# Moving a reflect-padding pass and its stores from one block of a kernel into the next, where other engines run beside it

## What is computed

```python
def gn(v, G=32, eps=1e-05):            # x: (4, 64, 56, 56)
    g = v.reshape(B, G, C // G, H, W)
    m, s = g.mean((2, 3, 4), keepdims=True), g.var((2, 3, 4), keepdims=True)
    return ((g - m) / sqrt(s + eps)).reshape(v.shape)

x1, x2, x3 = conv1x1(gn(x), w1c, b1c), conv1x1(gn(x), w2c, b2c), conv1x1(gn(x), w3c, b3c)
x2p = pad(x2, 3, mode='reflect')                      # 56x56 -> 62x62
diff = stack([x1 - x2p[:, :, dy:dy + H, dx:dx + W] for dy, dx in OFFS])   # 49 offsets
y = relu(bn(diff)); y = relu(bn(cw1 @ y)); wgt = softmax(cw2 @ y + cw2_b)  # over the 49 offsets
x3p = pad(x3, 3, mode='reflect')
out = sum(x3p[:, :, dy:dy + H, dx:dx + W] * wgt[:, :, k] for k, (dy, dx) in enumerate(OFFS))
x = x + out
```

## Time and profile before

| | |
|---|---|
| median of 3 runs | 1950.81 us (1948.31 to 1952.43) |
| the profiled execution: its time, its span | 1950.62 us, 1948.7 us |
| busy: PE, DVE, ACT, POOL | 1691.5, 1200.2, 1176.5, 696.9 us |
| first block, from start to barrier | 0 to 62 us |
| convolution's block, first subtraction | 62.00 us |
| first product of VectorE | 135.00 us |
| x3's stores issued, window loads issued | 57.06 us, 96.39 us |

### The profile page before, as it was taken

How to read it: one execution, slowest core, us unless ns; L and a number is a source line. 1 busy time by engine, 2 the same in 40 slices (tenths; PEclk the granted TensorE clock), 3 DMA queues, 4 the chain that set the end, 5 groups by cost and what they waited for, 6 DMA issues and landing times. The chain is left out here.

```text
span 1948.7 us, 33831 instructions
## 1 busy us (share of the span) xinstructions
PE 1691.5 (87%) x13143; PEld 622.7 (32%) x13143; DVE 1200.2 (62%) x1798; ACT 1176.5 (60%) x1605; POOL 696.9 (36%) x401
## 2 busy tenths in 40 slices
PE   4468778778765789999999999999897999999998
PEld 1011111111112434443433443344353334433333
DVE  3139999999985666666666666566265435453333
ACT  2799989989942445444444454444464556565664
POOL 0798978978856310000000000000130214332222
PEclk9799999999987689999999999999987999999999
DMA  2121211211221210000000000100121000010000
GB/s 98 82 101 48 84 37 48 84 44 41 84 95 70 87 34 16 16 15 15 16 16 13 14 15 16 46 15 16 22 79 32 8 5 8 8 41 8 8 10 9
DMA packets 27712, 73.27 MB, mean 38 GB/s; under 512 B 6968, under 2 KB 16184, under 8 KB 26160
## 3 DMA queue, kind: packets, MB, share of 16 engines
q1 hardware_dynamic: 27424, 70.31, 11.3%
q10 hardware_dynamic: 144, 0.96, 0.1%
HBM read 47.84 MB, written 13.62 MB: 32 GB/s over the span
## 5 line engine op out<-in xcount | busy, mean ns | idle before, releaser
L1362 DVE TENSOR_REDUCE at_mpart<-at_ps_m 128x1 f32<-128x384 f32 (+3 forms) x800 | 396.1, 556 | 167.8 <-PE at_ps_m L1072 167.3
L1215 ACT ACTIVATE at_prob<-at_ps_s 128x896 f32<-128x896 f32 x336 | 305.0, 917 | 317.3 <-PE at_ps_s L1090 309.4
L411 POOL TENSOR_TENSOR cm_diff<-front 128x1792 f32<-128x1792 f32 x98 | 320.5, 3274 | 68.9 <-POOLq L113 38.8
L477 DVE TENSOR_TENSOR cm_prod<-cm_ps_ev,win 128x1792 f32<-128x1792 f32 x168 | 333.0, 2018 | 5.3 <-ACT cm_ps_ev L531 1.3
L1881 ACT ACTIVATE ge_hid<-ge_ps,ffn 128x448 f32<-128x448 f32 x448 | 249.7, 634 | 122.1 <-PE ge_ps L1748 122.1
L1111 PE MATMUL at_ps_a<-at_prob,win 128*64 128x448 f32 x1344 | 292.0, 555 | 0.0
L1090 PE MATMUL at_ps_s<-vh,front 64*128 64x448 f16 x1344 | 253.6, 353 | 13.8 <-ACT at_prob L1215 7.8
L1090 PE MATMUL at_ps_s<-vl,front 64*128 64x448 f16 x1344 | 253.1, 352 | 0.0
L642 PE MATMUL cm_ps_acc<-cm_prod,cst 128*32 128x504 f32 x1456 | 197.4, 616 | 60.2 <-DVE cm_prod L477 26.9
L1010 POOL TENSOR_TENSOR attn<-attn 64x448 f32<-64x448 f32 x28 | 31.6, 1127 | 502.1 <-DMA attn<-attn 502.1
L1725 PE MATMUL ge_ps<-ge_hid,ffn 128*64 128x448 f32 x896 | 194.1, 554 | 0.5 <-DVE ge_part L2059 0.4
(11 more groups left out here) (228 smaller groups left out, 1964.2 us busy)
## 6 DMA issues: line engine op xcount, KB each, us to landing
win<-x_dram SPq DMA_DIRECT2D x28, 868.0 KB
at_rden<-rden_dram SPq DMA_DIRECT2D x28, 224.0 KB, 3.3
x_dram<-win SPq DMA_DIRECT2D x4, 962.0 KB
conv_out<-cm_cout SPq DMA_DIRECT2D x28, 112.0 KB, 3.9
win<-x SPq DMA_DIRECT2D x2, 1568.0 KB, 13.3
t_dram<-front SPq DMA_DIRECT2D x2, 1568.0 KB, 7.3
attn<-attn SPq DMA_DIRECT2D x28, 112.0 KB, 2.3
front<-t_dram SPq DMA_DIRECT2D x2, 1568.0 KB, 9.2
```

The lines of the kernel that those rows point to most:

```text
L411: pool.tensor_tensor(diff[:, s % ND, 0:n, :].rearrange("p n (r c) -> p n r c", c=W), a.rearrange("p n (r c) -> p n r c", c=W), b, ALU.subt ...
L477: v.tensor_tensor(halves_of(s)[:, hs, :, 0:CH].rearrange("p s (r c) -> p s r c", c=W), ev.rearrange("p s (r c) -> p s r c", c=W), window_o ...
L1215: act.activation(prob_of(s)[0:w, 0:a, :], ps_s[0:w, (s + 1 - par) % 2, 0:a, 0:CH], ACT.Exp).then_inc(exp_done, 1)
L1362: v.tensor_reduce(mpart[0:w, a, part:part + 1], ps_m[0:w, j % RB, 0:rough_columns(e)], AX.X, ALU.max).then_inc(rough_max, 1)
```

## The change

Five edits. (1) `x3`'s twelve mirror copies and the clearing of its last four columns leave VectorE's list in the first block and stand in the convolution's block, behind its two memsets and ahead of the first `running`. (2) The four stores of `x3` move with them: SyncE issues them in the second block, once `x3_padded` is raised. (3) `x2`'s mirror copies stay in the first block, but most are made while the last chunks of the 1x1 convolutions still run: sides of rows 0 to 47 and the top rows once chunk 5's `x2` is out, the sides of the last 8 rows and the bottom rows once chunk 6's is. (4) TensorE gets nine matmuls whose result nobody reads, six behind the transposition of `cw1` and three behind the matmul of the group means. (5) ScalarE gets an activation of one column as soon as `cst` is there, which brings its table load with it.

```diff
@@ conv_prepare
-                sp.wait_ge(padded, 1)
-                for b in range(B):
-                    dst = bass.AP(tensor=x3_dram.tensor, offset=b * NH * SP * STAGE,
-                                  ap=[[STAGE, 4], [SP * STAGE, NH], [4 * STAGE, 2], [1, STAGE]])
-                    sp.dma_start(dst, x3st[32 * b:32 * b + 32, :, :]).then_inc(x3_sent, 16)
                 sp.wait_ge(tok_in, 16)
...
-                v.wait_ge(evac_done, 4 * NCH)
-                x3v = x3st[:, :, 0:PADDED].rearrange("p s (r c) -> p s r c", c=WP)
                 x2v = x2p[:, :].rearrange("p (r c) -> p r c", c=WP)
-                v.memset(x3st[:, :, PADDED:STAGE], 0.0)
+                LATE = PAD + (NCH - 1) * ROWS
+
+                def sides(first, last):
+
+                    for d in range(PAD):
+                        for a, b in ((d, 2 * PAD - d), (WP - 1 - d, WP - 1 - 2 * PAD + d)):
+                            ins = v.tensor_copy(x2v[:, first:last, a], x2v[:, first:last, b])
+                    return ins
+
+                v.wait_ge(evac_done, 4 * (NCH - 2) + 2)
+                link(sides(PAD, LATE))
                 for d in range(PAD):
-                    for a, b in ((d, 2 * PAD - d), (WP - 1 - d, WP - 1 - 2 * PAD + d)):
-                        v.tensor_copy(x3v[:, :, PAD:PAD + H, a], x3v[:, :, PAD:PAD + H, b])
-                        ins = v.tensor_copy(x2v[:, PAD:PAD + H, a], x2v[:, PAD:PAD + H, b])
-                link(ins)
+                    v.tensor_copy(x2v[:, d, :], x2v[:, 2 * PAD - d, :])
+                v.wait_ge(evac_done, 4 * (NCH - 1) + 2)
+                link(sides(LATE, PAD + H))
                 for d in range(PAD):
-                    for a, b in ((d, 2 * PAD - d), (HP - 1 - d, HP - 1 - 2 * PAD + d)):
-                        ins = v.tensor_copy(x3v[:, :, a, :], x3v[:, :, b, :])
-                        v.tensor_copy(x2v[:, a, :], x2v[:, b, :])
-                ins.then_inc(padded, 1)
+                    v.tensor_copy(x2v[:, HP - 1 - d, :], x2v[:, HP - 1 - 2 * PAD + d, :])
...
+                act.wait_ge(c_in, 16)
+                act.activation(first[:, :], vec("b1"), ACT.Identity, bias=vec("b2"))
                 act.wait_ge(bn_ready, 1)
...
+                def keep_running(times):
+
+                    for _ in range(times):
+                        pe.matmul(psx[:, 1, 3, 0:CH], mat("ident"), cst[:, 0:CH], start=True, stop=True)
+
                 pe.transpose(psx[:, 1, 0, 0:128], cwt[:, :], mat("ident")).then_inc(cw_turned, 1)
+                keep_running(6)
                 pe.wait_ge(moments, 1)
                 pe.matmul(psx[:, 0, 0, 0:4], mat("pair_mean"), mom[:, :, :].rearrange("p t m -> p (t m)"),
                           start=True, stop=True).then_inc(grouped, 1)
+                keep_running(3)
@@ conv_main
+                sp.wait_ge(x3_padded, 1)
+                for b in range(B):
+                    dst = bass.AP(tensor=x3_dram.tensor, offset=b * NH * SP * STAGE,
+                                  ap=[[STAGE, 4], [SP * STAGE, NH], [4 * STAGE, 2], [1, STAGE]])
+                    sp.dma_start(dst, x3st[32 * b:32 * b + 32, :, :]).then_inc(x3_sent, 16)
                 sp.wait_ge(x3_sent, 64)
...
                 v.memset(hid[96:128, 1, :, :], 0.0).then_inc(lanes_done, 1)
                 v.memset(rden_d[:, :, :], 0.0).then_inc(lanes_done, 1)
+                x3v = x3st[:, :, 0:PADDED].rearrange("p s (r c) -> p s r c", c=WP)
+                v.memset(x3st[:, :, PADDED:STAGE], 0.0)
+                for d in range(PAD):
+                    for a, b in ((d, 2 * PAD - d), (WP - 1 - d, WP - 1 - 2 * PAD + d)):
+                        ins = v.tensor_copy(x3v[:, :, PAD:PAD + H, a], x3v[:, :, PAD:PAD + H, b])
+                ins.then_inc(x3_sides, 1)
+                v.wait_ge(x3_sides, 1)
+                for d in range(PAD):
+                    for a, b in ((d, 2 * PAD - d), (HP - 1 - d, HP - 1 - 2 * PAD + d)):
+                        ins = v.tensor_copy(x3v[:, :, a, :], x3v[:, :, b, :])
+                ins.then_inc(x3_padded, 1)
                 for T in TURNS:
```

More of the change, by code:

```diff
@@ L60, with conv_prepare @@
     ["b1", "b2", "b3a", "b3b", "g1", "t1", "m1", "v1", "g2", "t2", "m2", "v2", "cw2b", "cw2b3", "mhalf"])}
-def conv_prepare(nc, x, consts, tok_c, cst, tok, x1, x2p, x3st, x3_dram, x3_sent):
+def conv_prepare(nc, x, consts, tok_c, cst, tok, x1, x2p, x3st):
     with ExitStack() as ctx:
@@ L84, in conv_prepare @@
         tmp = sb("cp_tmp", [128, 4])
+        first = sb("cp_first", [128, 1])
         psx = ctx.enter_context(nc.psum_tensor("cp_psx", [128, 2, 4, BANK], F32))
@@ L100, in conv_prepare @@
         evac_done = sem("cp_evac_done")
-        padded = sem("cp_padded")
         CUTS = (slice(0, 4 * CH), slice(4 * CH, PIX))
@@ L238, in _, with conv_main @@
                     ins.then_inc(conv_done, 1)
-def conv_main(nc, x, cst, front, win, x3_dram, x3_sent, conv_out, tres_in, last_in, early_added):
+def conv_main(nc, x, cst, front, win, x3st, x3_dram, x3_sent, conv_out, tres_in, last_in, early_added):
     with ExitStack() as ctx:
@@ L294, in conv_main @@
         pool_prod_done = sem("cm_pool_prod_done")
+        x3_sides = sem("cm_x3_sides")
+        x3_padded = sem("cm_x3_padded")
         N = NCH * STEPS
@@ L2203, in build @@
             x3st = win_flat[:, 0:2 * STAGE].rearrange("p (s n) -> p s n", s=2)
-            conv_prepare(nc, x, conv_c, tok_c, cst, tok, front[:, 0:PIX], front[:, PIX:PIX + PADDED], x3st, x3_dram,
-                         x3_sent)
-            conv_main(nc, x, cst, front, win, x3_dram, x3_sent, conv_out, tres_in, last_in, early_added)
+            conv_prepare(nc, x, conv_c, tok_c, cst, tok, front[:, 0:PIX], front[:, PIX:PIX + PADDED], x3st)
+            conv_main(nc, x, cst, front, win, x3st, x3_dram, x3_sent, conv_out, tres_in, last_in, early_added)
         tres = tokens_of_front(front)
```

## The result

The changed kernel takes **1965.1 us** (median of 4 runs, 1961.61 to 1967.9) against 1951.62 of four runs before: 1.0071 times as long, with a 95% interval of 1.0057 to 1.0085. That is 13.5 us slower. The profiled execution took 1961.61 us, with a span of 1959.6.

What follows compares the result with a forecast made beforehand. The prediction took VectorE as bound from the first product on, and the window's data chain ahead of it. First product +15.4 and restart 0.8 made +16.2 on 1950.62: 1966.8 us, between 1963.5 and 1971 (1952 to 1971 for 8 in 10).

Steps and rivals of the forecast that it cites:

- S: Time SyncE issues the first store of x3: 57.06 in the kernel before, forecast at 73.4 us.
- the compute chain: From GpSimd's first subtraction through ScalarE's first exponential to VectorE's first product: 73.0 us from block start.
- the first law: Data chain of x3's stores and window loads: first product no earlier than S + 77 us (75.3 to 77.9).
- Taking turns: In the convolution's block, one VectorE copy passes per GpSimd subtraction until subtraction 5 ends: S = 73.4; chance 0.72.
- the burst case: Rival: x3's copies wait for GpSimd only once per group; S = 60.5, whole 1953.2 us; chance 0.12.
- the free case: Rival: x3's copies don't wait for GpSimd at all; S = 57.0, whole 1949.7 us; chance 0.09.
- My doubt about them: Whether x3's column copies take turns with GpSimd; if only the six rows do, S = 72.5 instead of 73.4.
- Block start: GpSimd's first subtraction in the convolution's block: forecast 52.2 us (51.5 to 53.5) instead of 62.00.
- The waking: Extra matmuls and early activation before the 1x1 convolutions: last evacuation 2.3 us earlier (1.0 to 3.0).
- Handovers: Six copies let in between GpSimd's first six subtractions: 0.7 us added to their 19.3.
- the leftovers: Copies left after subtraction 5, the semaphore and six rows, passing freely on VectorE before the stores: 1.2 us.
- The restart: TensorE back at the slow clock after idling before the first product: 0.8 us added (0 to 3).

Runs made afterwards that it cites:

- e1: The changed kernel, but GpSimd's first subtraction waits until x3's copies are made; median 1948.43 us, ratio 0.9996 to the kernel before.
- e2: The changed kernel, but GpSimd makes only its first two subtractions before x3's copies are done; one execution, 1954.34 us.
- e3: The changed kernel, with x3's clearing and copies ahead of the block's two memsets on VectorE; one execution, 1967.78 us.
- e4: The changed kernel, with x3's twelve copies written as four instructions of the same elements; median 1957.26 us, ratio 1.0039 to the kernel before.
- e8: The changed kernel, with 24 unread matmuls on TensorE ahead of the first product's sums; one execution, 1963.72 us.
- e6: The changed kernel, with x3's copies back in the first block and only the stores in the second; median 1946.44 us, ratio 0.9977 to the kernel before.
- e5: The kernel before, with only the nine extra matmuls and the early activation added; median 1947.84 us, ratio 0.9984.
- e7: e6 with the top rows stored and the first window loaded before the rest, staging tile at win's other end; median 1941.57 us, ratio 0.9958.
- e9: e7 with only the last eight rows of x3 mirrored in the second block, in three merged copies; median 1940.87 us, ratio 0.9954.

## Why the prediction was right

**The frame.** The product starts at S + 77 or at block start + 73, whichever is later. In seven kernels the window decided, in four the compute chain:

| kernel | S | behind S | block start | behind it |
|---|---|---|---|---|
| after | 71.42 | **76.95** | 50.89 | 97.48 |
| e1 | 55.26 | **77.00** | 55.31 | 76.95 |
| e2 | 59.24 | **76.86** | 50.97 | 85.13 |
| e3 | 71.46 | **77.27** | 50.92 | 97.81 |
| e4 | 64.06 | **77.00** | 50.63 | 90.43 |
| e8 | 71.33 | **77.10** | 50.78 | 97.65 |
| e6 | 52.55 | **77.07** | 52.58 | 77.04 |
| e5 | 53.71 | 77.91 | 58.64 | **72.98** |
| e7 | 54.16 | (stores cut) | 54.19 | **72.98** |
| e9 | 50.79 | (stores cut) | 50.81 | **73.68** |

(The kernel before, at 77.94 and 73.00, makes the fourth.) In e1 and e6 the store and the block's start fall together: the product comes 77 behind both, where the compute chain takes 73, and its row names the DMA. So the first law isn't the compute chain in disguise. The 77 had been put together from a rate and a count without any row for the fourth load's landing; it held to 0.3.

**Taking turns.** This was the step with the rivals, and it held in kind and nearly in size. Six column copies ended behind six subtractions, the rows passed when GpSimd ran dry, and zero, two, four and six turns gave S = 55.26, 59.24, 64.06 and 71.42. So the burst case (S = 60.5) and the free case (57.0) fall with the trace of the changed kernel, and e1 to e4 exclude that something else held the copies. All six column copies waited, one subtraction each. My doubt about them, drawn from their slow pace, was wrong; it had been priced at 0.9 us. By the Trainium skill (VectorE: DVE Perf Modes, What auto-detection actually checks) a copy from SBUF to SBUF whose outermost dimension is even takes a 2-port mode, and in such a mode it contends with GpSimd for a port pair that whichever issues first holds for the whole instruction (SBUF — State Buffer, Who interferes with whom). The trace agrees, with six waits of six.

**Sizes.** Forecast +16.2 to the 25th product, measured +14.24, and 13.5 between the medians. The terms:

- Block start, 52.2 forecast, 50.89 measured, 0.6 outside its bound of 51.5. The waking had been taken at 2.3 between 1.0 and 3.0, for fear of the clock falling again before the convolutions. It gave 3.12 at the last evacuation, which began at 49.44 (52.56 before). e5 gives 3.36 for both chains. The barrier had been put 0.8 behind the last evacuation; it took 0.29 (50.60 to 50.89), so the 0.77 that stood between the stores' issue and the barrier before was no constant of the barrier. Together 1.3 of the 2.0 missing from S.
- Handovers: 0.7 had been added for six copies let in between; the six subtractions took 19.45 against 19.3, so 0.15. This is 0.5 more. The last 0.15 of the 2.0 is in the leftovers, 1.08 us for 1.2.
- The restart, 0.8 forecast, 0.87 measured. e8 removes it by keeping TensorE busy and so shows the cause. That the size came out so well is luck: the other kernels that stood still lose 0.58 (e3), 1.14 (e1), 1.27 (e4), 1.58 (e2) and 1.59 (e6) up to the 25th product, and not the more the longer they stood (e6 3.98 us, the changed kernel 18.00). What sets it is open.
- The range: the bounds named in the prediction's sum add up to 1962.7 to 1971.2, not to 1963.5 to 1971. The median, 1965.1, lies in both. The profiled execution, 1961.61, lies in neither; of the 5.2 us between it and 1966.8, some 2.0 are S and 3.2 the shorter stretch from attention on, which the sum had as unchanged.

**Where the early block went.** The 11.1 us are real, and e5, e6, e7 and e9 bring 3.4, 5.4, 7.8 and 10.5 of such gains to the first product. In the changed kernel the compute chain would have been ready for the product long before 148.37, and stood still for 18.00 us.

Two things the working had loose. It put the stall at "more like 15"; it was 18.00, since the running maximum is further into the compute chain than assumed. In e9 it came 14.18 behind the block's start without being held up by the copies; in the changed kernel, at 71.31, it was 6.2 late for that, which leaves 148.37 - (50.89 + 73.0 + 6.2) = 18.3. And the profiled execution's span rose by 10.91 only, because attention ran shorter in it; the marks ahead of attention, +14.14, are nearer to the 13.5 between the medians.

## What to carry to other kernels

Work moved to run "beside" another engine is not hidden when the two share a lock: read from the trace what each short instruction took beside the neighbour's long ones, and count the instructions, since here each of them paid a turn as long as the neighbour had work (all but one pair), and not each element. Before moving the start of a block, work out every chain that ends at the first instruction that must not be late, with its slack: here the window was full at 57.06 + 77.0 = 134.1 by the runs, 0.9 us ahead of the product at 135.00 (the prediction had allowed up to 2.6), so an early start was worth that alone and, beyond it, a late store cost one for one. And put a producer's copies where the neighbour is idle, and send first what is needed first: splitting the stores in two took e7 another 4.0 us ahead of e6 at the 25th product (1.6 of it the restart that e7 doesn't pay), 4.9 between the medians.

## What the runs showed of the hardware

A turn isn't lost by every instruction: in e9 two copies of 48 elements of each partition, issued together, passed in one gap, where copies of 112 never did while a subtraction was due (14 of them waited one by one: six each in the changed kernel and in e3, two in e2; so did those of 336 in e4). Whether size or timing decides was not tried.

Matmuls without a reader don't fix where TensorE's slow stretch falls. Windows of 28 to 31 us, in the 1x1 convolutions, of before, after and e7:

```profile
28.00:31.00 3.00, 3.00 (x10) 0.96 (x10) 0.00 (x0) 0.00 (x0) 0.00 (x0) 1.00 0.00 0
```

```profile
28.00:31.00 3.00, 3.00 (x18) 1.14 (x16) 0.00 (x0) 0.78 (x2) 0.00 (x0) 1.00 0.00 0
```

```profile
28.00:31.00 3.00, 3.00 (x14) 1.03 (x12) 0.00 (x0) 0.00 (x0) 0.00 (x0) 0.67 0.00 0
```

In the changed kernel the slow stretch fell ahead of the convolutions (granted clock 0.57 in 21 to 25, where it costs little: their first matmul starts at 25.42, in e7 at 24.83), in e7 into them (0.76 in 25 to 28, 0.67 here), and its first evacuation came at 31.61, where the other nine kernels with these matmuls have it at 29.98 to 30.31. The row of before is the odd one: it reads 1.00, and yet shows 10 matmuls in 3 us where the changed kernel has 18 at the same reading, and weight loads 0.75 us apart where later ones of the same kernel are 0.38 apart. So I read the level there from the pace of the matmuls, 1.2 GHz before and 2.4 after, and not from the clock's column.
